# A post-norm transformer layer on eight cores: transposes for the second half of the tokens issued before the first half's down-projection, and residual buffers moved to make room

## The reference

```python
# x: (8, 2048, 2048) float32
x = layernorm(x + attn(x, wq, wk, wv, wo))       # 16 heads of 128, rope on half of each head, softmax over all keys
x = layernorm(x + ffn(x, ...))
# ffn, HID = 5632; the weights are integers 0..255 with one scale for each output row
qlinear(x, wq, s) = x @ ((wq - 128) * s[:, None]).T
ffn(x) = qlinear(silu(qlinear(x, wq_gate, s_gate)) * qlinear(x, wq_up, s_up), wq_down, s_down)
```

## Time and profile before

| | us |
|---|---|
| median of 3 runs | 4667.8 (4665.5 to 4864.3) |
| the profiled execution | 4655.4 |
| its span, slowest core | 4653.2 |
| spans of the eight cores | 4640.4 to 4653.5 |

### The profile page before, as it was taken

How to read it: one execution, slowest core, us unless ns; L and a number is a source line. 1 busy time by engine, 2 the same in 40 slices (tenths; PEclk the granted TensorE clock), 3 DMA queues, 4 the chain that set the end, 5 groups by cost and what they waited for, 6 DMA issues and landing times.

```text
span 4653.2 us, 41524 instructions; the slowest of 8 cores (4640.4 to 4653.5 us)
## 1 busy us (share of the span) xinstructions
PE 3816.7 (82%) x15368; PEld 1484.3 (32%) x15680; DVE 608.3 (13%) x1312; ACT 1309.2 (28%) x1061; POOL 357.9 (8%) x680
## 2 busy tenths in 40 slices
PE   4999997777777777777957999988862999997882
PEld 1444442111111111112423444433320444443331
DVE  0222100001000100001310000011220000001112
ACT  0111113343334334433442333310014333330004
POOL 1000000000000000000000000012210000002220
PEclk8999998788888877888978999999985999999996
DMA  7334321100110010011574444334446434435444
GB/s 131 60 68 98 82 67 38 28 14 14 23 19 14 14 28 14 14 19 38 184 192 74 78 73 81 73 78 63 59 82 147 79 73 81 73 57 89 64 62 129
DMA packets 200710, 310.94 MB, mean 67 GB/s; under 512 B 99265, under 2 KB 152642, under 8 KB 191682
## 3 DMA queue, kind: packets, MB, share of 16 engines
q0 software_dynamic: 97344, 188.85, 25.1%
q1 hardware_dynamic: 98562, 115.22, 8.2%
q10 hardware_dynamic: 4608, 4.20, 0.3%
HBM read 412.86 MB, written 58.72 MB: 101 GB/s over the span
## 4 chain that ended last, share of the span: by engine, by line
PE 68%; DMA 16%; issue 6%; ACT 5%; DVE 4%; another core or an unknown queue 0%; DVEq 0%; SPq 0%; ACTq 0%; POOL 0%; POOLq 0%
PE PS L595 13%; PE PS L602 13%; PE PS L488 9%; DMA AB<-wd_c 9%; PE PS L540 6%; PE PS L536 5%; PE PS L573 5%; PE PS L503 5%; PE PS L525 4%; PE PS L616 3%; ACT AB L661 3%; PE PS L528 3%; DMA AB<-AB 3%; DMA AB<-x1b 2%; DMA AB<-xT 2%
## 5 line engine op out<-in xcount | busy, mean ns | idle before, releaser
L661 ACT ACTIVATE AB<-PS,AB 128x1024 bf16<-128x1024 f32 x512 | 563.9, 1113 | 852.0 <-PE PS L528 825.4
L595 PE MATMUL PS<-AB 128*128 128x512 bf16 x2759 | 621.1, 380 | 203.9 <-DMA AB<-x1b 201.0
L616 PE MATMUL PS<-AB 128*128 128x512 bf16 x2760 | 652.5, 387 | 112.5 <-DVE AB L818 107.4
L602 PE MATMUL PS<-AB 128*128 128x512 bf16 x2760 | 618.7, 379 | 2.9
L488 PE MATMUL PS<-AB 128*128 128x512 bf16 x2008 | 446.5, 383 | 66.8 <-DMA AB<-xT 64.5
L525 PE MATMUL PS<-AB 128*128 128x512 bf16 x497 | 239.7, 482 | 285.5 <-DVE AB L765 271.3
L595 PEld LDWEIGHTS PS<-AB 128*128 128x128 bf16 x2816 | 275.9, 98 | 535.5 <-issue 205.3
L616 PEld LDWEIGHTS PS<-AB 128*128 128x128 bf16 x2816 | 266.2, 99 | 498.8 <-issue 228.7
L536 PE MATMUL PS<-AB 128*128 128x512 bf16 x869 | 381.0, 438 | 36.8 <-ACT AB L661 35.8
L540 PE MATMUL PS<-AB 128*1 128x512 bf16 x896 | 377.2, 421 | 8.4 <-issue 4.4
L602 PEld LDWEIGHTS PS<-AB 128*128 128x128 bf16 x2816 | 275.6, 98 | 332.2
(11 more groups left out here) (74 smaller groups left out, 1693.3 us busy)
## 6 DMA issues: line engine op xcount, KB each, us to landing
AB<-wg_c POOLq DMA_DIRECT2D x88, 512.0 KB, 5.1
AB<-wu_c POOLq DMA_DIRECT2D x88, 512.0 KB, 7.1
AB<-wd_c POOLq DMA_DIRECT2D x352, 128.0 KB, 2.9
AB<-x SPq DMA_DIRECT2D x16, 1024.0 KB, 5.9
x1f<-AB SPq DMA_DIRECT2D x16, 1024.0 KB, 3.9
AB<-x1f SPq DMA_DIRECT2D x16, 1024.0 KB, 5.0
out<-AB SPq DMA_DIRECT2D x16, 1024.0 KB, 5.7
AB<-xT POOLq DMA_DIRECT2D x16, 512.0 KB, 13.3
```

The source lines that it names most:

```text
L595: mm = t.matmul(bank(par * 4 + cch)[:, 0:512], GDQ[par][:, di * 128:(di + 1) * 128], X1T[:, di * 1024 + cch * 512: di * 1024 + (cch + 1) * ...
L602: mm = t.matmul(bank(par * 4 + 2 + cch)[:, 0:512], UDQ[par][:, di * 128:(di + 1) * 128], X1T[:, di * 1024 + cch * 512: di * 1024 + (cch + ...
L616: mm = t.matmul(bank(tt)[:, 0:512], HT[:, h2 * 1024 + tt * 128: h2 * 1024 + (tt + 1) * 128], WDQ[i % 2][:, 0:512], start=(h2 == 0), stop=( ...
L661: sc.activation(PT[u % 4], bank(2 * (u % 2), 2)[:, 0:1024], AF.Exp, bias=CVC[:, 0:1], scale=ASCL).then_inc(s2sc, 1)
```

## The change

XR8 moves up by 32768 bytes: its eight blocks now lie over HT blocks 0 to 31 (four HT blocks under each), and none over X1T. With that:

- SP issues the transposes of the second half right behind those of the first, when the gate and up matmuls of the first half are done (s4pe). The x1f loads of each half are gated one by one in the last down-projection pass: XR8[g8] is loaded when PE has used HT blocks up to 4 * g8 + 3 in pass dc = 3.
- PE waits for each transposed block where the first tile of a half first uses it, not for all sixteen. Before tile 44 it waits for the evictions (s4de 32), which was implied before.
- ACT dequantizes tile 44 behind the squares of the first half and before the square root, not behind the normalizations.
- DVE waits for the store of XR8[ht // 4] before it writes HT blocks 0, 4, ..., 28 of the second half (before: blocks 0, 4, 8, 12, for XR8[4..7]).

```diff
--- before.py
+++ after.py
@@ -166,7 +166,7 @@
     WOT = QT
 
     XRS = [f32(OFF_XRES + i * 8192, 128, 2048) for i in range(2)]
-    XR8 = [f32(g * 8192, 128, 2048) for g in range(8)]
+    XR8 = [f32(32768 + g * 8192, 128, 2048) for g in range(8)]
     S4B = f32(OFF_STAT4, 128, 80)
     ROU = [f32(OFF_ROUT + i * 8192, 128, 2048) for i in range(3)]
     X1O = [f32(OFF_X1O + i * 8192, 128, 2048) for i in range(3)]
@@ -353,12 +353,10 @@
                     if DEBUG:
                         s.wait_ge(s0d, 16 * 2 * NH)
                 else:
-                    s.wait_ge(s4out[0], 16 * 2)
-                    s.wait_ge(s4out[1], 16 * 2)
+                    s.wait_ge(s4pe, 2 * NHT)
+                    s.wait_ge(s3spb, 16 * NT)
                 for dt in range(NDI):
                     gi = th * NDI + dt
-                    if th == 1 and dt == 0:
-                        s.wait_ge(s3spb, 16 * NT)
                     if gi >= 2:
                         s.wait_ge(s4xt[gi % 2], 16 * (gi // 2))
                     s.dma_start_transpose(
@@ -367,12 +365,10 @@
                     ).then_inc(s4xt[gi % 2], 16)
                 if th == 0:
                     s.wait_ge(s3spf, 16 * NT)
+            for th in range(2):
                 for g8 in range(8):
                     g = th * 8 + g8
-                    if g8 == 0:
-                        s.wait_ge(s4pe, 2 * NHT * (th + 1))
-                    if g8 == 4:
-                        s.wait_ge(s4dn, 4 * NHT * (th + 1))
+                    s.wait_ge(s4dn, (th * 4 + 3) * NHT + 4 * g8 + 4)
                     if g >= 1:
                         s.wait_ge(s4x, 16 * g)
                     s.dma_start(out=XR8[g8], in_=x1f[g * 128:(g + 1) * 128, :]).then_inc(s4x, 16)
@@ -579,8 +575,6 @@
                 return
             t.wait_ge(s3ra, NT)
             for th in range(2):
-                t.wait_ge(s4xt[0], 16 * (NDI // 2) * (th + 1))
-                t.wait_ge(s4xt[1], 16 * (NDI // 2) * (th + 1))
                 if th == 0:
                     t.wait_ge(s3spf, 16 * NT)
                     t.wait_ge(s3spb, 16 * NT)
@@ -589,8 +583,12 @@
                     t.wait_ge(s4dq, 2 * (i + 1))
                     if i >= 2:
                         t.wait_ge(s4stt, i - 1)
+                    if ht == 0 and th == 1:
+                        t.wait_ge(s4de, 32)
                     par = i % 2
                     for di in range(NDI):
+                        if ht == 0:
+                            t.wait_ge(s4xt[di % 2], 16 * (th * 8 + di // 2 + 1))
                         for cch in range(2):
                             mm = t.matmul(bank(par * 4 + cch)[:, 0:512],
                                           GDQ[par][:, di * 128:(di + 1) * 128],
@@ -693,7 +691,7 @@
             sc.wait_ge(s3sq, NT)
             for th in range(2):
                 for it in range(NHT + 1):
-                    if it < NHT:
+                    if it < NHT and not (th == 1 and it == 0):
                         i = th * NHT + it
                         sc.wait_ge(s4w[i % 2], 32 * (i // 2 + 1))
                         if i >= 2:
@@ -718,6 +716,14 @@
                                   bias=zero_b, scale=1.0, accum_out=S4B[:, g8:g8 + 1])
                     sc.activation(DSB[:, g8 * 2048:(g8 + 1) * 2048], XR8[g8], AF.Square,
                                   accum_out=S4B[:, 8 + g8:9 + g8]).then_inc(s4sq, 1)
+                if th == 0:
+                    i0 = NHT
+                    sc.wait_ge(s4sq, 8)
+                    sc.wait_ge(s4w[0], 32 * (i0 // 2 + 1))
+                    sc.wait_ge(s4pe, 2 * (i0 - 1))
+                    sc.activation(GDQ[0], GBF[0], AF.Identity, bias=CVC[:, 1:2], scale=1.0)
+                    sc.activation(UDQ[0], UBF[0], AF.Identity, bias=CVC[:, 1:2],
+                                  scale=1.0).then_inc(s4dq, 2)
                 sc.wait_ge(s4v1, th + 1)
                 sc.activation(S4B[:, 48:56], S4B[:, 40:48], AF.Sqrt)
                 sspace(sc)
@@ -799,8 +805,8 @@
             for th in range(2):
                 for ht in range(NHT):
                     i = th * NHT + ht
-                    if th == 1 and ht % 4 == 0 and ht <= 12:
-                        go = 4 + ht // 4
+                    if th == 1 and ht % 4 == 0 and ht <= 28:
+                        go = ht // 4
                         v.wait_ge(s4out[go % 2], 16 * (go // 2 + 1))
                     v.wait_ge(s4sil, i + 1)
                     v.wait_ge(s4pe, 2 * i + 2)
```

## The result

| | before | after |
|---|---|---|
| ratio of the runs, 95% interval | 1 | 0.9919 (0.9898 to 0.9941) |
| profiled execution, us | 4655.4 | 4631.7 |
| its span, slowest core | 4653.5 | 4630.1 |
| mean span of its eight cores | 4647.4 | 4616.2 |

The ratio makes 38 us of 4667.8: about 4630 us, where 4619 was forecast. The slowest core of the profiled execution shows 23 us (the 4653.2 given for the kernel before is core 0; core 6 took 4653.5), the mean of the cores 31, so single cores are no good measure of a few microseconds. (In some executions the cores of one die or both run at a lower clock whatever the kernel; they are left out.)

What follows compares the result with a forecast made beforehand. It took PE as the main bound, the down-projection as paced by two wd buffers. Boundary -64.7, start -6, x1f loads +14, transposes +8 gave -48.7 us, from 4667.8 to 4619 us; range 4596 to 4648 us.

Steps and rivals of the forecast that it cites:

- The boundary: Between the halves: PE restarts 73.5 us earlier, less a second stop of 6.5 and a slow restart of 2.3; 64.7 us less.
- rival (d): Between the halves: PE's restart stays late; if it waits for normalization, some 10 us of gain go, 4629 us; chance 0.03.
- The start of the first half: First gate matmuls: PE follows the transposes one by one instead of waiting for all; 6 us less, bounds 0 and 7.4.
- Part 3: Down-projection: four x1f loads leave the first quarter, eight enter the last, at 1.7 us each; 14 us more in all.
- Part 4: Down-projection of the first half: second-half transposes run beside wd loads; 8 us more, bounds 3 and 20.
- one-for-one turns: Transposes beside wd loads: the queues alternate packet by packet, 0.45 us a pair of blocks, 14 pairs, 6 us.
- longer turns: Transposes beside wd loads: engines change queue only after packets of typically 9 to 17 descriptors, making the cost 20 us.
- The clock: Last quarter of the down-projection: PE's granted clock falling because of gaps made by the loads would show the prediction wrong.
- Rival (a): Down-projection: contention eats most of the gain, loads at 3.1 us each and transposes at 20; 4653 us, chance 0.17.
- (b): Down-projection: contention is free, spaced loads at 0.8 us each and transposes 3; 4600 us or lower, chance 0.14.
- (c): Last quarter of the down-projection: each x1f load holds the wd stream 5.5 us; slower than before, 4680 us, chance 0.04.

## Why the prediction was off where it was

- **The boundary, right.** Forecast: PE restarts 73.5 us earlier, stops for 6.5 us, starts slowly for 2.3: 64.7 us. Measured by the means: restart 71.6 earlier, tile 45 6.8 later, the 43 tiles behind it 2.3 longer: 62.5 us. Each wait was ended by what was named, and putting the dequantization back cost 9.5 us where its rival (d) said some 10.
- **The start of the first half, right.** 6 us forecast, 5.3 measured (5 to 8 over the runs with the same start).
- **The x1f loads, mis-sized.** The step that failed is in Part 3, "I take the measured 1.7, since it is the same load beside the same stream". The first passes, freed of four loads, gained 7.0 us in the second half (6.6 forecast). The last passes paid 21.4 and 18.5, not 13.6: 2.7 and 2.3 us a load. It took the price of one place for another: the 1.7 came from four pairs at the very start of a pass, and the same group of four released in the middle of a pass cost 10.3 and 10.2 us, 2.6 each. That the two blocks already loaded when a pass starts make the difference is likely, but no run shows it. The upper bound of Part 3, a load's 3.1 us of work on the engines, was nearer. The earlier trace rows had told why: DVE waited for wd_c in 306 of 352 blocks, so little could absorb a delay; with four buffers both the wait and the cost went. This is 12.7 of the 18 us missing between 48.7 and the 31 of the means. The first pass of the first half brings 3.1 more, the boundary 2.2, the start 0.7.
- **The transposes, near by luck.** Part 4 took 8 us; it was 10 (the first pass rose by 4.5 in the first half, 1.4 forecast). But the 8 was 14 pairs of blocks at 0.45 us, and 2 on top. The transposes ran through in 41 us, in which 15 wd loads were issued: 7 to 8 pairs, so some 1.4 us a pair. The price of a packet was right, the count of turns was not. The two queues in 3073 to 3140 of the changed kernel, then in the four microseconds 3096 to 3100:

```profile
q0 software_dynamic: 3888, 3.54, 46.6%
q1 hardware_dynamic: 16472, 4.09, 42.3%
...
q0 software_dynamic: 248, 0.24, 65.7%
q1 hardware_dynamic: 246, 0.05, 58.6%
```

  Over the whole stretch a transpose packet took 0.423 x 67 x 16 / 16472 = 27.5 ns, the 28 of the prediction, and there were four of them for one of wd. The short stretch alone has equal counts, as the earlier trace rows had, and 152 ns a packet, but it holds 246 of the 16384 packets, and 22 of these make 87% of its time; the stretches of 4 us beside it have 1529 and 2102. So neither the one-for-one turns nor the longer turns of which the Trainium skill speaks (DMA: Bandwidth & Descriptors, section Queues, rings and completion order) are shown by these counts, and why it is 10 stays open. The upper bound was low as well: at 27.5 ns the packets are 28 us of the engines' time and not 20. The shares of the two queues add up to over 100% in the short stretch, so that the time of a record is not all work of its own.
- **The clock, a sign that came true.** The prediction named a falling clock in the last passes as a sign of being wrong. The mean granted clock of the eight cores there was 0.98 in both halves before, and 0.94 and 0.96 after (stretches at full clock and stretches at half, the lower of its two levels, taken together); with all eight loads moved out it was 0.97 and 0.98 again, with four buffers 0.98. The length of the pass times the share not granted rises by 4.8 and 2.0 us, which is, as an estimate, the most that the clock can have in the 21.4 and 18.5. No run separates it from the waits, and it went with them.
- **Rival (a)**, contention near the bounds, was the mechanism of the miss, at a little under half its strength: the contention forecast was 22 us, (a) had 56, and by the means it was 37 (62.5 + 5.3 - 31). Rivals (b) and (c) fall: no load was free, and none cost 4.7 us.
- **What was not asked at all.** The prediction called the down-projection paced by two buffers in its first part and then priced each contention inside that pace. It did not ask what the pace itself costs: 88 against 78 us a pass, eight times.

## What to carry to other kernels

A stream that its consumer waits for on nearly every round has little slack. The 1 MB loads put beside it here were paid at 2.3 to 2.7 us each, spaced, shifted or in groups, and at some 3.1 cut into pieces, with 3.1 us of work; the transposes at 10 of 28. Price such a transfer nearer to its work than to the cheapest stretch seen. Before moving transfers into such a stage give the stream more buffers: two more of 128 KB here were worth 105 us by themselves and made the moved transfers nearly free. Where a chain of waits falls away, ask which instruction of the last engine in it can be moved for the second tile too.

## What was not expected of the hardware

- With four buffers the down-projection runs at 76 to 78 us a pass though its loads still take 3.0 us each and the DMA engines do more in less time: the two-buffer stream left them half idle (busy share about 0.5 in undisturbed passes, 0.58 beside x1f loads).
- Cutting a 1 MB load into pieces with 2 KB rows brought the median wd load beside it from 4.1 to 3.0 us, and the pass did not become shorter.
- Packets of DMA transposes took 28 ns beside gate and up loads and 27.5 ns on average beside wd loads, but unevenly: in 3096 to 3100 half of the 246 took 18 ns or less and the longest 1.5 us.
